# Output stage of an adaLN block: attention numerators loaded in the layout of the product, inverted sums spread over head rows by TensorE

## The chip, the cores and the metric

One Trainium2 chip (trn2); the program runs on 1 core. The metric is the device time of one execution in microseconds (us), the median of three runs.

## The reference, cut to what matters

The block normalises x, runs causal attention with 16 heads of 16 columns, adds a gated attention output to x, and then runs a small mixture-of-experts step on the first two batches. What the change touches is the end of the attention:

```python
B, L, D = 16, 1024, 256          # batches, tokens, columns; 16 heads x 16
probs = softmax(scores)          # the kernel keeps numerators and sums apart
out = einsum('bhij,bhjd->bhid', probs, v)
out = out.transpose(0, 2, 1, 3).reshape(B, L, D)
out = out @ Wo + bo
x = x + ga * (h + out)           # h: the modulated layer norm of x
```

All of it is float32.

## The kernel before, in words

The kernel is a row of blocks, each ended by all engines: `phase0` (tables, weights), `phase1` (norms, q, k, v), `phase2` (scores, exp, weighted sums), `phase3` (the output stage), `phase4` (experts). Only `phase3` changes, with one more tensor in DRAM.

`phase2` leaves `att_d[b, g]`, 128 rows of 1024 tokens for each of four groups of four heads. A head has 32 rows: 16 numerators, then its sum of exponentials (row 16, `DH`), and 15 unused ones. So heads and columns are rows, and tokens are along the free dimension.

`phase3` works through B = 16 batches of T = 8 tiles of 128 tokens. For each batch SyncE loads `gate`, `ob` (three bf16 parts of a bias) and `att` (2 MB, two buffers; L1122 to L1125), and three to four batches ahead x and `a2` (L1127 to L1131). It stores a batch once all eight tiles are added (L1135 to L1137), and issues the next loads behind that store.

Per tile TensorE transposes the four groups of `att` into one PSUM bank, 128 tokens by 512 (L1230). VectorE takes the reciprocal of the 16 sums (L1166) and multiplies the numerators by it into `norm`, 128 by 256 (L1170). TensorE transposes `norm` in two pieces (L1238), ScalarE copies them to `n_t` (L1199), and TensorE adds up a bias matmul (L1248, bf16) and two float32 matmuls of `n_t` with `wg` (L1250). `wg` is `Wo` times the batch's gate, two VectorE products at the batch's start (L1159). VectorE adds the residual (L1177). The residual `res` comes from ScalarE (L1189) and two GpSimd products (L1213, L1215), up to a batch ahead. The three steps of a tile are staggered by one tile each on TensorE, within a batch: the loop over `T + 2` steps starts and ends anew in each batch. A float32 matmul shows as two instructions in the trace, a transposition as one.

The order of the work is written out by hand: each engine has its own queue, and semaphores set who waits.

Of the kernel before, what the change touches and what calls it, by code (L numbers as in the profile page):

```python
# [17 lines left out]
F32 = mybir.dt.float32  # L18
# [3 lines left out]
ALU = mybir.AluOpType  # L22
# [38 lines left out]
def build(nc, a, out):  # L61
# [20 lines left out]
    att_d = nc.dram_tensor("att", [B, NG, P, L], F32, kind="Internal").ap()  # L82
    tok_d = nc.dram_tensor("tok_rows", [SEL, D + E], F32, kind="Internal").ap()
    sum_d = nc.dram_tensor("sum_rows", [SEL + P, D], F32, kind="Internal").ap()

    with ExitStack() as outer:
# [19 lines left out]
        phase3(nc, x, ps, ident, wo, ones3, rsx, nmx, mods_d, out_bias_d, att_d, sum_d, out)  # L106
# [975 lines left out]
def phase3(nc, x, ps, ident, wo, ones3, rsx, nmx, mods_d, out_bias_d, att_d, sum_d, out):  # L1082
# [3 lines left out]
    DH = D // HEADS  # L1086
    SB = (sum_d.shape[0] - P) // L
    PS_A, PS_T, PS_C = 0, 2, 4
    XR = 4
    with ExitStack() as ctx:  # L1090
# [3 lines left out]
        att = sb("att_b", [P, 2, NG, L], F32)  # L1094
        xb = sb("x_b", [P, XR, T, D], F32)
        res = sb("res_b", [P, 2, T, D], F32)
        gate = sb("gate_b", [P, 2, D], F32)
        a2 = sb("a2_b", [P, XR, D], F32)
        ob = sb("ob_b", [3, 2, D], BF16)
        wg = sb("wg", [P, 2, KC, D], F32)  # L1100
        rec = sb("rec", [P, 2, HEADS], F32)
        norm = sb("norm", [P, 2, D], F32)
        n_t = sb("n_t", [P, 2, KC, P], F32)
        x2 = sb("x2", [P, 2, T, D], F32)
        att_in, small_in = pair("p3_att_in"), pair("p3_small_in")
        x_in = tuple(sem(f"p3_x_in{r}") for r in range(XR))
        r_norm, r_mul, r_done = sem("p3_r_norm"), sem("p3_r_mul"), sem("p3_r")
        wg_done = sem("p3_wg")
        at_done, rec_done, norm_done = sem("p3_at"), sem("p3_rec"), sem("p3_norm")
        nt_done, nt_copied = sem("p3_nt"), sem("p3_nt_copied")  # L1110
# [4 lines left out]
        def loop(eng, work):  # L1115
            for p in range(2):
                work(p, 0, p)
            for it in range(1, B // 2):
                for p in range(2):
                    work(it * 2 + p, it, p)  # L1120

        def load(sp, b, p):  # L1122
            sp.dma_start(gate[:, p], mods_d[b, M_GA, :].partition_broadcast(P)).then_inc(small_in[p], DMA)
            sp.dma_start(ob[:, p], out_bias_d[b]).then_inc(small_in[p], DMA)
            sp.dma_start(att[:, p], att_d[b].rearrange("g p t -> p g t")).then_inc(att_in[p], DMA)  # L1125

        def load_x(eng, b):  # L1127
            r = b % XR
            reuse(eng, r_done, (b - XR) * T + T)
            eng.dma_start(xb[:, r], x[b].rearrange("(t p) d -> p t d", p=P)).then_inc(x_in[r], DMA)  # L1130
            eng.dma_start(a2[:, r], mods_d[b, M_A2, :].partition_broadcast(P)).then_inc(x_in[r], DMA)  # L1131

        @block.sync
        def _(sp):
            def store(b, p, dst):  # L1135
                sp.wait_ge(x2_done, b * T + T)
                sp.dma_start(dst.rearrange("(t p) d -> p t d", p=P), x2[:, p]).then_inc(stored[p], DMA)  # L1137

            load(sp, 0, 0)
            load_x(sp, 0)  # L1140
            load(sp, 1, 1)
            for b in range(1, XR):
                load_x(sp, b)
            for b in range(B):
                if b + XR - 1 < B and b >= 1:
                    load_x(sp, b + XR - 1)
                store(b, b % 2, sum_d[b * L:(b + 1) * L] if b < SB else out[b])
                if b + 2 < B:
                    load(sp, b + 2, b % 2)
            for p in range(2):  # L1150
                sp.wait_ge(stored[p], DMA * (B // 2))

        @block.vector
        def _(dve):
            def work(b, half, p):
                dve.wait_ge(small_in[p], half * (2 * DMA) + 2 * DMA)
                reuse(dve, stored[p], half * DMA)
# [3 lines left out]
                for t in range(T + 2):  # L1161
                    if t < T:
                        s = t % 2
                        dve.wait_ge(at_done, b * T + t + 1)
                        heads = ps[:, PS_A + s, :].rearrange("p (h n) -> p h n", h=HEADS)
                        dve.reciprocal(rec[:, s, :].rearrange("p (h o) -> p h o", o=1), heads[:, :, DH:DH + 1]) \  # L1166
                           .then_inc(rec_done, 1)
                        dve.wait_ge(rec_done, b * T + t + 1)
                        reuse(dve, nt_done, b * T + t - 1)
                        dve.tensor_tensor(norm[:, s, :].rearrange("p (h n) -> p h n", h=HEADS), heads[:, :, 0:DH],  # L1170
                                          rec[:, s, :].rearrange("p (h o) -> p h o", o=1).to_broadcast([P, HEADS, DH]),
                                          ALU.mult).then_inc(norm_done, 1)
                    if t >= 2:
                        s = t % 2
                        dve.wait_ge(c_done, b * T + t - 1)
                        dve.wait_ge(r_done, b * T + t - 1)
                        dve.tensor_tensor(x2[:, p, t - 2, :], ps[:, PS_C + s, 0:D], res[:, p, t - 2, :], ALU.add) \  # L1177
                           .then_inc(x2_done, 1)

            loop(dve, work)  # L1180

        @block.scalar
        def _(act):
            def first_norm(b, t):
                p = b % 2
                if t == 0:
                    act.wait_ge(x_in[b % XR], (b // XR + 1) * 2 * DMA)
                    reuse(act, x2_done, b * T - T)
                nc.scalar.activation(res[:, p, t, :], xb[:, b % XR, t, :], ACT.Identity, bias=nmx[:, b, t:t + 1],  # L1189
                                     scale=rsx[:, b, t:t + 1]).then_inc(r_norm, 1)  # L1190

            def work(b, half, p):
                for t in range(T):
                    n = b * T + t + 2
                    if n < B * T:
                        first_norm(n // T, n % T)
                    act.wait_ge(nt_done, b * T + t + 1)
                    reuse(act, c_done, b * T + t - 1)
                    nc.scalar.copy(n_t[:, t % 2], ps[:, PS_T + t % 2, 0:D].rearrange("p (k n) -> p k n", k=KC)) \  # L1199
                      .then_inc(nt_copied, 1)  # L1200

            for t in range(2):
                first_norm(0, t)
            loop(act, work)
# [16 lines left out]
        @block.tensor  # L1221
        def _(pe):
            def work(b, half, p):
                pe.wait_ge(att_in[p], half * DMA + DMA)
                for t in range(T + 2):
                    s = t % 2
                    if t < T:
                        reuse(pe, norm_done, b * T + t - 1)
                        for g in range(NG):
                            ins = pe.transpose(ps[:, PS_A + s, g * P:(g + 1) * P], att[:, p, g, t * P:(t + 1) * P],  # L1230
                                               ident[:, :])
                        ins.then_inc(at_done, 1)
                    if 1 <= t <= T:
                        r = t - 1
                        pe.wait_ge(norm_done, b * T + r + 1)
                        reuse(pe, nt_copied, b * T + r - 1)
                        for k in range(KC):
                            ins = pe.transpose(ps[:, PS_T + r % 2, k * P:(k + 1) * P],  # L1238
                                               norm[:, r % 2, k * P:(k + 1) * P], ident[:, :])
                        ins.then_inc(nt_done, 1)  # L1240
                    if t >= 2:
                        r = t - 2
                        if r == 0:
                            pe.wait_ge(wg_done, b + 1)
                        pe.wait_ge(nt_copied, b * T + r + 1)
                        reuse(pe, x2_done, b * T + r - 1)
                        o = ps[:, PS_C + r % 2, 0:D]
                        pe.matmul(o, ones3[:, :], ob[:, p, :], start=True, stop=False)  # L1248
                        for k in range(KC):
                            ins = pe.matmul(o, n_t[:, r % 2, k, :], wg[:, p, k, :], start=False, stop=(k == KC - 1))  # L1250
                        ins.then_inc(c_done, 1)

            loop(pe, work)


# [368 lines left out]
```

## Time and profile before

| | us |
|---|---|
| median of 3 runs (lowest, highest) | 3128.5 (3128.36, 3128.82) |
| the profiled execution, its own time | 3130.67 |
| its span in the profile | 3128.6 |
| PE / DVE / ACT / POOL busy over the span | 2768.8 / 2213.2 / 1818.1 / 1060.7 |
| `phase3`: first transfer issued / last addition ended | 2501.9 / 2782.6 |

PE is TensorE, PEld its weight loads, DVE VectorE, ACT ScalarE, POOL GpSimd, SP SyncE (SPq its queue of transfers). Times in rows are microseconds from the start of the span unless marked ns. The busy shares are means over stages that have different limits; for a change in one stage its own windows and timeline are what to read.

### The profile page before, as it was taken

Reading aid. Unit: us, or ns where it says so; the run is one execution under the profiler, and the core shown is the slowest. Engines: PE = TensorE matmul, PEld = TensorE weight load, DVE = VectorE, ACT = ScalarE, POOL = GpSimd, SP = SyncE. Lnnn points to the kernel's source line nnn. Section 1 sums busy time; section 2 is a strip of 40 time slices with the busy share of each in tenths; the row PEclk is TensorE's granted clock in tenths of the full one; section 3 lists DMA queues with packets and bytes.
Section 4 is the critical chain, followed back from the end, with each engine's and each line's share of the span. In section 5 each row is a group of like instructions: output and inputs, shape, how many; then the busy total and the mean of one; then the engine's idle time right before and its main releaser. Section 6 shows DMA issues by size and latency. Waiting matters only on the chain. (4 is left out here: it accounts for less than half of the span.)

```text
span 3128.6 us, 48266 instructions
## 1 busy us (share of the span) xinstructions
PE 2768.8 (88%) x17467; PEld 1343.6 (43%) x17467; DVE 2213.2 (71%) x3164; ACT 1818.1 (58%) x3723; POOL 1060.7 (34%) x1294
## 2 busy tenths in 40 slices
PE   1677777669999999999999999999999889957997
PEld 0444444324444444444444444444444267744664
DVE  4999999867777777777777777777777245552221
ACT  1655656507777777777777777777777634421121
POOL 1787778421122111211122112212122166642231
PEclk7899899859999999999999999999999989988999
DMA  3366665663444454444444454445444087752342
GB/s 93 118 195 188 200 200 155 215 132 73 104 92 91 93 104 100 89 89 103 104 90 89 97 104 96 91 90 104 100 92 89 22 286 266 268 189 82 83 115 45
DMA packets 188549, 386.18 MB, mean 123 GB/s; under 512 B 33413, under 2 KB 104485, under 8 KB 175800
## 3 DMA queue, kind: packets, MB, share of 16 engines
q1 hardware_dynamic: 182170, 374.58, 46.7%
q0 software_dynamic: 6144, 8.52, 1.6%
q8 instruction: 141, 2.31, 0.3%
q14 instruction: 94, 0.77, 0.1%
HBM read 240.65 MB, written 144.53 MB: 123 GB/s over the span
## 5 line engine op out<-in xcount | busy, mean ns | idle before, releaser
L922 DVE TENSOR_REDUCE mx<-ps 128x2 f32<-128x1024 f32 (+3 forms) x1216 | 1371.6, 1167 | 397.7 <-PE ps L1010 302.4
L968 ACT ACTIVATE prob<-ps 128x512 f32<-128x512 f32 (+1 forms) x2560 | 1251.7, 560 | 539.8 <-PE ps L1028 531.0
L1003 PE MATMUL ps<-k_rows,q_rows 96*128 96x512 bf16 (+3 forms) x3072 | 910.9, 332 | 47.2 <-DMA k_rows<-k_parts 40.6
L1028 PE MATMUL ps<-q_rows,k_rows 99*128 99x512 bf16 (+3 forms) x3072 | 907.4, 329 | 14.2 <-ACT prob L968 5.8
L861 POOL TENSOR_SCALAR_AFFINE_SELECT prob<-prob 128x512 f32<-128x512 f32 x512 | 318.7, 634 | 1452.9 <-ACT prob L968 1452.9
L1047 PE MATMUL ps<-prob,v_rows 128*32 128x512 f32 (+3 forms) x6144 | 628.8, 497 | 0.0
L1028 PEld LDWEIGHTS ps<-q_rows,k_rows 99*128 99x128 bf16 x3072 | 273.1, 98 | 599.1 <-ACT prob L968 360.0
L1003 PEld LDWEIGHTS ps<-k_rows,q_rows 96*128 96x128 bf16 x3072 | 289.8, 98 | 277.7 <-DVE mx L922 60.8
L1010 PE MATMUL ps<-mask_b,unit_b 128*128 128x128 bf16 (+2 forms) x1408 | 348.6, 248 | 0.0
L666 PE MATMUL ps<-x_t,w_all 128*128 128x512 f32 x512 | 248.5, 631 | 0.0
L1047 PEld LDWEIGHTS ps<-prob,v_rows 128*32 128x32 f32 x6144 | 134.4, 108 | 246.1 <-ACT prob L968 123.3
L655 PE MATMUL ps<-ident,h 128*128 128x128 f32 x256 | 55.2, 317 | 151.2 <-ACT x_t L567 82.5
L628 POOL TENSOR_TENSOR h<-xin,mods_b 128x256 f32<-128x256 f32 x128 | 146.0, 1143 | 106.9 <-ACT xin L552 106.8
L635 POOL TENSOR_TENSOR stage<-rest,stage 128x1024 bf16<-128x1024 f32 x64 | 147.5, 2306 | 35.5 <-ACT stage L588 35.4
L1484 DVE SCALAR_TENSOR_TENSOR y<-ps,gx,gate 128x256 f32<-128x256 f32 x32 | 15.5, 484 | 195.9 <-PE ps L1575 195.9
L1010 PEld LDWEIGHTS ps<-mask_b,unit_b 128*128 128x128 bf16 x1408 | 139.5, 99 | 22.8
L1250 PE MATMUL ps<-wg,n_t 128*128 128x256 f32 x512 | 146.6, 409 | 0.0
L666 PEld LDWEIGHTS ps<-x_t,w_all 128*128 128x128 f32 x512 | 101.8, 207 | 104.1 <-issue 103.2
L1199 ACT COPY n_t<-ps 128x256 f32<-128x256 f32 x128 | 47.5, 371 | 155.2 <-PE ps L1238 155.2
L1177 DVE TENSOR_TENSOR x<-ps,res_b 128x256 f32<-128x256 f32 x128 | 54.4, 425 | 109.5 <-PE ps L1250 109.5
L674 PE MATMUL ps<-w_all,x_t 128*128 128x256 f32 x512 | 126.1, 390 | 3.3 <-ACT v_st L576 2.0
L1213 POOL TENSOR_TENSOR res_b<-res_b,a_b 128x256 f32<-128x256 f32 x128 | 93.0, 727 | 85.2 <-ACT res_b L1189 85.2
(154 smaller groups left out, 2777.6 us busy)
## 6 DMA issues: line engine op xcount, KB each, us to landing
k_rows<-k_parts SPq DMA_DIRECT2D x384, 128.0 KB, 7.3
v_ones<-v_st SPq DMA_DIRECT2D x64, 512.0 KB, 4.3
v_rows<-v_ones SPq DMA_DIRECT2D x64, 512.0 KB, 9.1
att<-o_sb SPq DMA_DIRECT2D x128, 256.0 KB, 2.5
att_b<-att SPq DMA_DIRECT2D x16, 2048.0 KB, 9.9
q_parts<-stage SPq DMA_DIRECT2D x128, 192.0 KB, 3.3
k_parts<-stage SPq DMA_DIRECT2D x128, 192.0 KB, 3.3
q_rows<-q_parts SPq DMA_DIRECT2D x64, 384.0 KB, 4.6
```

What stands on the lines that cost most here:

```text
L628: pool.tensor_tensor(h[:, p, t, :], xin[:, r, t, :], mods[:, r, M_CA1, :], ALU.mult).then_inc(h_mul, 1)
L635: pool.tensor_tensor(parts(n, 2), rest[:, n % 2], parts(n, 1), ALU.subtract).then_inc(lo_done, 1)
L666: ins = pe.matmul(ps[:, PS_QK + c, :], w_all[:, k, c * P:(c + 1) * P], x_t[:, blk, k, :], start=(k == 0), stop=(k == KC - 1))
L674: ins = pe.matmul(o, x_t[:, t // 4, k, t % 4 * P:t % 4 * P + P], w_all[:, k, 2 * D:3 * D], start=(k == 0), stop=(k == KC - 1))
L861: pool.affine_select(out=own, in_=own, compare_op=ALU.is_ge, fill=0.0, base=0, pattern=[[0, HG], [1, P]], channel_multiplier=-1).then_inc( ...
L922: dve.tensor_reduce(dst, src, AX.X, ALU.max).then_inc(a_free, 1)
L968: nc.scalar.activation(prob[:, (g * NPC + i) % RING, h, 0:w], src, ACT.Exp).then_inc(exp_done, 1)
L1003: ins = pe.matmul(ps[:, at, col:col + w], q[0:ROWS, g, h, i * P:(i + 1) * P], k[0:ROWS, g, h, k0:k0 + w], start=(r == 0), stop=True, skip_ ...
L1010: ins = pe.matmul(own, unit_b[:, :], mask_b[:, :].rearrange("p (o n) -> p o n", o=1) .to_broadcast([P, per, P]), start=False, stop=True, s ...
L1028: ins = pe.matmul(ps[:, PS_B + bank(g, n), at:at + w], k[0:AUG, g, h, j * P:(j + 1) * P], q[0:AUG, g, h, q0:q0 + w], start=True, stop=True)
L1047: ins = pe.matmul(ps[32 * h:32 * h + 32, PS_O, col:col + w], v[:, g, j, h, :], prob[:, (g * NPC + i) % RING, h, at:at + w], start=(j == 0) ...
L1250: ins = pe.matmul(o, n_t[:, r % 2, k, :], wg[:, p, k, :], start=False, stop=(k == KC - 1))
```

## The change

Instead of loading all rows of a batch's `att` and turning them twice, the stage loads only the numerators, so that the 256 rows of (head, column) fill 128 partitions twice (`num`, 1 MB in two transfers), and the sums apart (`den`: 16 sums of 1024 tokens as 128 rows of 128). VectorE inverts the sums in one instruction per batch; SyncE stores the inverses to DRAM (`rec_d`) and loads them back as 16 rows of 1024 (`rec`). TensorE multiplies a 0/1 matrix (`head_rows`, 16 by 256) by `rec`, which puts each head's inverse on its 16 rows, 512 tokens per matmul, four per batch, two PSUM banks. VectorE multiplies `num` by that bank into `n_t`, which has the layout that the product wants. The product itself is the same three matmuls per tile, now with four PSUM banks.

The spreads and products of batch b+1 are interleaved with the products of batch b: on TensorE one after every second product, on VectorE one after every second addition. `wg` of batch b+1 is made on VectorE at the start of batch b (before: at its own start), from a `gate` that is still loaded behind the store of batch b-1. SyncE's order is new (the listing has it). ScalarE has only the residual left, whose wait is now per tile. In the diff, removed bodies (printed above) are left out.

```diff
@@ build @@
+    rec_d = nc.dram_tensor("rec_sums", [B, HEADS, L], F32, kind="Internal").ap()
...
@@ phase3 @@
+    HALF = L // 2
+    PS_R, PS_C = 0, 2
+    XR, CR = 4, 4
+    NQ = 2 * KC
...
+        num = sb("num", [P, 2, KC, L], F32)
+        den = sb("den", [P, 2, P], F32)
+        inv = sb("inv", [P, 2, P], F32)
+        rec = sb("rec", [HEADS, 2, L], F32)
+        rows = sb("head_rows", [HEADS, HEADS, DH], F32)
+        n_t = sb("n_t", [P, 2, KC, L], F32)
...
         @block.sync
         def _(sp):
...
+            def load_den(b):
+                reuse(sp, inv_done, b - 1)
+                sums = att_d[b].rearrange("g (h n) t -> (g h) n t", n=2 * DH)[:, DH, :]
+                sp.dma_start(den[:, b % 2, :], sums.rearrange("h (a c) -> h a c", c=P)).then_inc(den_in[b % 2], DMA)
+            def save_inv(b):
+                sp.wait_ge(inv_done, b + 1)
+                sp.dma_start(rec_d[b].rearrange("h (a c) -> (h a) c", c=P), inv[:, b % 2, :]).then_inc(inv_stored[b % 2], DMA)
+            def load_rec(b):
+                sp.wait_ge(inv_stored[b % 2], (b // 2 + 1) * DMA)
+                reuse(sp, spread, (b - 1) * NQ)
+                sp.dma_start(rec[:, b % 2, :], rec_d[b]).then_inc(rec_in[b % 2], DMA)
+            def load_num(b):
+                reuse(sp, norm_done, (b - 1) * NQ)
+                for k in range(KC):
+                    mine = att_d[b, k * NG // KC:(k + 1) * NG // KC].rearrange("g (h n) t -> (g h) n t", n=2 * DH)
+                    sp.dma_start(num[:, b % 2, k, :], mine[:, 0:DH, :]) \
+                      .then_inc(num_in[b % 2], DMA)
+            def load_x(b):
+                r = b % XR
+                reuse(sp, r_done, (b - XR) * T + T)
+                sp.dma_start(xb[:, r], x[b].rearrange("(t p) d -> p t d", p=P)).then_inc(x_in[r], DMA)
+                sp.dma_start(a2[:, r], mods_d[b, M_A2, :].partition_broadcast(P)).then_inc(x_in[r], DMA)
+            def load_small(b):
+                reuse(sp, c_done, (b - 1) * T)
+                sp.dma_start(gate[:, b % 2], mods_d[b, M_GA, :].partition_broadcast(P)).then_inc(small_in[b % 2], DMA)
+                sp.dma_start(ob[:, b % 2], out_bias_d[b]).then_inc(small_in[b % 2], DMA)
+            def store(b):
                 sp.wait_ge(x2_done, b * T + T)
...
+                dst = sum_d[b * L:(b + 1) * L] if b < SB else out[b]
+                sp.dma_start(dst.rearrange("(t p) d -> p t d", p=P), x2[:, b % 2]).then_inc(stored[b % 2], DMA)
+            load_den(0)
+            load_den(1)
+            load_num(0)
+            load_small(0)
+            save_inv(0)
+            load_x(0)
+            load_rec(0)
+            save_inv(1)
+            load_num(1)
+            load_rec(1)
+            load_small(1)
+            load_den(2)
+            load_x(1)
+            load_x(2)
             for b in range(B):
...
                 if b + 2 < B:
...
+                    save_inv(b + 2)
+                if b + 3 < B:
+                    load_den(b + 3)
+                    load_x(b + 3)
+                if b + 2 < B:
+                    load_num(b + 2)
+                    load_rec(b + 2)
+                store(b)
+                if b + 2 < B:
+                    load_small(b + 2)
             for p in range(2):
                 sp.wait_ge(stored[p], DMA * (B // 2))
         @block.vector
         def _(dve):
...
+            def invert(b):
+                dve.wait_ge(den_in[b % 2], (b // 2 + 1) * DMA)
+                reuse(dve, inv_stored[b % 2], b // 2 * DMA)
+                dve.reciprocal(inv[:, b % 2, :], den[:, b % 2, :]).then_inc(inv_done, 1)
+            def scale_weights(b):
+                p = b % 2
+                dve.wait_ge(small_in[p], (b // 2 + 1) * 2 * DMA)
                 for k in range(KC):
                     ins = dve.tensor_tensor(wg[:, p, k, :], wo[:, k, :], gate[:, p, :], ALU.mult)
                 ins.then_inc(wg_done, 1)
...
+            def normalise(b, q):
+                k, half = q % KC, q // KC
+                at = slice(half * HALF, (half + 1) * HALF)
+                if q == 0:
+                    dve.wait_ge(num_in[b % 2], (b // 2 + 1) * KC * DMA)
+                    reuse(dve, c_done, (b - 1) * T)
+                dve.wait_ge(spread, b * NQ + q + 1)
+                dve.tensor_tensor(n_t[:, b % 2, k, at], num[:, b % 2, k, at], ps[:, PS_R + q % 2, :], ALU.mult) \
+                   .then_inc(norm_done, 1)
+            def finish(b, t):
+                n = b * T + t
+                if t == 0:
+                    reuse(dve, stored[b % 2], b // 2 * DMA)
+                dve.wait_ge(c_done, n + 1)
+                dve.wait_ge(r_done, n + 1)
+                dve.tensor_tensor(x2[:, b % 2, t, :], ps[:, PS_C + n % CR, 0:D], res[:, b % 2, t, :], ALU.add) \
+                   .then_inc(x2_done, 1)
+            dve.tensor_copy(rows[:, :, :], ident[0:HEADS, 0:HEADS].rearrange("p (h o) -> p h o", o=1)
+                            .to_broadcast([HEADS, HEADS, DH])).then_inc(rows_done, 1)
+            for b in range(2):
+                invert(b)
+            scale_weights(0)
+            for q in range(NQ):
+                normalise(0, q)
+            for b in range(B):
+                if b + 2 < B:
+                    invert(b + 2)
+                if b + 1 < B:
+                    scale_weights(b + 1)
+                for t in range(T):
+                    finish(b, t)
+                    if t % 2 == 1 and b + 1 < B:
+                        normalise(b + 1, t // 2)
         @block.scalar
         def _(act):
                 p = b % 2
                 if t == 0:
                     act.wait_ge(x_in[b % XR], (b // XR + 1) * 2 * DMA)
-                    reuse(act, x2_done, b * T - T)
+                reuse(act, x2_done, (b - 2) * T + t + 1)
                 nc.scalar.activation(res[:, p, t, :], xb[:, b % XR, t, :], ACT.Identity, bias=nmx[:, b, t:t + 1],
                                      scale=rsx[:, b, t:t + 1]).then_inc(r_norm, 1)
...
+            for b in range(B):
                 for t in range(T):
...
+                    first_norm(b, t)
         @block.gpsimd
         def _(pool):
         @block.tensor
         def _(pe):
...
+            def spread_rec(b, q):
+                k, half = q % KC, q // KC
+                n = b * NQ + q
+                if q == 0:
+                    pe.wait_ge(rec_in[b % 2], (b // 2 + 1) * DMA)
+                reuse(pe, norm_done, n - 1)
+                mine = rows[:, k * (HEADS // KC):(k + 1) * (HEADS // KC), :].rearrange("p h n -> p (h n)")
+                pe.matmul(ps[:, PS_R + q % 2, :], mine, rec[:, b % 2, half * HALF:(half + 1) * HALF],
+                          start=True, stop=True).then_inc(spread, 1)
+            def product(b, t):
+                n = b * T + t
+                if t == 0:
+                    pe.wait_ge(wg_done, b + 1)
+                if t in (0, T // 2):
+                    pe.wait_ge(norm_done, b * NQ + (KC if t == 0 else NQ))
+                reuse(pe, x2_done, n - CR + 1)
+                o = ps[:, PS_C + n % CR, 0:D]
+                pe.matmul(o, ones3[:, :], ob[:, b % 2, :], start=True, stop=False)
+                for k in range(KC):
+                    ins = pe.matmul(o, n_t[:, b % 2, k, t * P:(t + 1) * P], wg[:, b % 2, k, :], start=False,
+                                    stop=(k == KC - 1))
+                ins.then_inc(c_done, 1)
+            pe.wait_ge(rows_done, 1)
+            for q in range(NQ):
+                spread_rec(0, q)
+            for b in range(B):
+                for t in range(T):
+                    product(b, t)
+                    if t % 2 == 0 and b + 1 < B:
+                        spread_rec(b + 1, t // 2)
```

## Rows read from the trace of the kernel before

**Rows 1.** Window, steady part: us, PE PEld DVE ACT POOL busy, PEclk, DMA share, GB/s
```profile
2533.99:2782.56 248.57, 234.02 (x1316) 176.44 (x1314) 140.11 (x391) 101.35 (x237) 168.09 (x234) 1.00 0.73 247
```

**Rows 2.** Timeline of TensorE, one tile: start, us, engine, line
```profile
2539.47 0.60 PE L1230 MATMUL ps<-ident,att_b 128*128 128x128 f32 x4
...
2540.22 0.28 PE L1248 MATMUL ps<-ob_b,ones 3*128 3x256 bf16 x1
...
2540.43 1.13 PE L1250 MATMUL ps<-wg,n_t 128*128 128x256 f32 x4
...
2541.40 0.60 PE L1230 MATMUL ps<-ident,att_b 128*128 128x128 f32 x4
```

**Rows 3.** Timeline at a batch's edge, all engines
```profile
2547.49 0.28 PE L1248 MATMUL ps<-ob_b,ones 3*128 3x256 bf16 x1
...
2548.77 0.28 PE L1248 MATMUL ps<-ob_b,ones 3*128 3x256 bf16 x1
...
2550.14 0.42 DVE L1177 TENSOR_TENSOR x<-ps,res_b 128x256 f32<-128x256 f32 x1 [0.85 <-PE ps L1250]
...
2550.48 0.75 DVE L1159 TENSOR_TENSOR wg<-wo,gate_b 128x256 f32<-128x256 f32 x2
...
2550.59 0.36 SPq L1137 DMA_DIRECT2D sum_rows<-x  x1
...
2551.00 0.58 SPq L1123 DMA_DIRECT2D gate_b<-mods  x1
...
2551.62 1.13 SPq L1124 DMA_DIRECT2D ob_b<-out_bias_parts  x1
...
2551.92 0.44 PE L1238 MATMUL ps<-ident,norm 128*128 128x128 f32 x2 [0.94 <-DVE norm L1170]
```

**Rows 4.** Critical chain, one row; groups by form, three: count | busy us, mean ns | idle
```profile
2875.96 12.03 PE ps L1561 x28
...
L1439 DVE TENSOR_TENSOR same<-ps,idxf 128x512 f32<-128x512 f32 x8 | 5.5, 692 | 0.9 <-PE ps L1538 0.4
...
L266 DVE RECIPROCAL e<-e 16x256 f32<-16x256 f32 x1 | 1.7, 1742 | 0.0
...
L1166 DVE RECIPROCAL rec<-ps 128x16 f32<-128x16 f32 x128 | 32.8, 256 | 13.7 <-PE ps L1230 12.6
```

**Rows 5.** Windows after E = 2683.15; landings of L1137, then of L1125
```profile
2683.15:2687.15 4.00, 3.06 (x22) 2.38 (x21) 2.78 (x9) 1.63 (x4) 1.17 (x2) 1.00 0.78 268
2683.15:2688.15 5.00, 4.06 (x26) 3.07 (x25) 3.62 (x11) 2.24 (x6) 2.15 (x3) 1.00 0.75 232
...
2688.60:2689.10 0.50, 0.50 (x6) 0.49 (x5) 0.29 (x1) 0.00 (x0) 0.50 (x2) 1.00 0.89 98
...
2690.15:2692.15 2.00, 2.00 (x13) 1.56 (x12) 1.11 (x3) 0.94 (x3) 1.72 (x3) 1.00 1.02 422
...
2697.60:2698.10 0.50, 0.50 (x3) 0.09 (x1) 0.09 (x1) 0.01 (x1) 0.50 (x2) 1.00 0.40 135
...
DMA to landing us min/median/max: 4.1/4.8/5.1
...
DMA to landing us min/median/max: 8.3/9.9/14.5
```

**Rows 6.** Timeline of the stage's start, and a window of it
```profile
2501.88 0.32 SPq L1123 DMA_DIRECT2D gate_b<-mods  x1
...
2505.09 0.76 DVE L1159 TENSOR_TENSOR wg<-wo,gate_b 128x256 f32<-128x256 f32 x2 [57.43 <-DMA ob_b<-out_bias_parts]
...
2510.90 1.97 PE L1230 MATMUL ps<-ident,att_b 128*128 128x128 f32 x8 [12.18 <-DMA att_b<-att]
...
2517.38 2.08 PE L1250 MATMUL ps<-wg,n_t 128*128 128x256 f32 x4
...
2523.86 1.13 PE L1250 MATMUL ps<-wg,n_t 128*128 128x256 f32 x4
...
2502.00:2520.00 18.00, 6.80 (x25) 5.39 (x26) 3.23 (x9) 3.10 (x7) 3.98 (x6) 0.51 0.86 310
```

More of the change, by code:

```diff
@@ L105, in build @@
         phase2(nc, B, L, ps, ident, mask, q_d, k_d, v_d, max_d, att_d)
-        phase3(nc, x, ps, ident, wo, ones3, rsx, nmx, mods_d, out_bias_d, att_d, sum_d, out)
+        phase3(nc, x, ps, ident, wo, ones3, rsx, nmx, mods_d, out_bias_d, att_d, rec_d, sum_d, out)
         phase4(nc, a, SB, ps, ident, mask, ones3, mods_d, b2_d, tok_d, sum_d, out)
@@ L1078, in _, with phase3 @@
                 weigh(unit(LAST, NG - 1), i)
-def phase3(nc, x, ps, ident, wo, ones3, rsx, nmx, mods_d, out_bias_d, att_d, sum_d, out):
+def phase3(nc, x, ps, ident, wo, ones3, rsx, nmx, mods_d, out_bias_d, att_d, rec_d, sum_d, out):
     B, L, D = x.shape
@@ L1113, in phase3 @@
         block = ctx.enter_context(nc.Block())
[L1115 to L1131, printed above, removed]
         @block.sync
         def _(sp):
-            def store(b, p, dst):
-                sp.wait_ge(x2_done, b * T + T)
[L1137 to L1143, printed above, removed]
+            def load_den(b):
+                reuse(sp, inv_done, b - 1)
+                sums = att_d[b].rearrange("g (h n) t -> (g h) n t", n=2 * DH)[:, DH, :]
+                sp.dma_start(den[:, b % 2, :], sums.rearrange("h (a c) -> h a c", c=P)).then_inc(den_in[b % 2], DMA)
@@ L1144, in _ @@
+            load_small(1)
+            load_den(2)
+            load_x(1)
+            load_x(2)
             for b in range(B):
-                if b + XR - 1 < B and b >= 1:
-                    load_x(sp, b + XR - 1)
-                store(b, b % 2, sum_d[b * L:(b + 1) * L] if b < SB else out[b])
                 if b + 2 < B:
-                    load(sp, b + 2, b % 2)
+                    save_inv(b + 2)
[8 more added lines that the diff above has]
+                    load_small(b + 2)
@@ L1154, in _ @@
         def _(dve):
-            def work(b, half, p):
-                dve.wait_ge(small_in[p], half * (2 * DMA) + 2 * DMA)
-                reuse(dve, stored[p], half * DMA)
+            def invert(b):
[5 more added lines that the diff above has]
+                dve.wait_ge(small_in[p], (b // 2 + 1) * 2 * DMA)
                 for k in range(KC):
@@ L1160, in work @@
                 ins.then_inc(wg_done, 1)
[L1161 to L1178, printed above, removed]
@@ L1180, in _ @@
-            loop(dve, work)
+            def normalise(b, q):
[7 more added lines that the diff above has]
+                   .then_inc(norm_done, 1)
@@ L1222, in _ @@
         def _(pe):
[L1223 to L1251, printed above, removed]
```

27 lines of the change are left out of this document (4 added, 23 removed).

## The prediction

> **What bounds the kernel now.** I read the windows by stage first. The output stage works from the end of batch 0 (2533.99) to the end of batch 15 (2782.56) with TensorE busy 234.0 of 248.6 us at a granted clock of 1.00 (2.4 GHz, the higher of its two levels), the DMA engines 73%, the other engines 68% or less [rows 1]: 15 batches of 16.57 us each. Nothing of the stages before or after overlaps it, since each stage is a block of its own, so what a batch loses the kernel loses.
>
> Next the timeline of one tile in the steady part. From one tile's first transposition to the next one's there are 1.93 us, and TensorE fills them: transpositions of `att_b`, of `norm`, the bias matmul, and the product, which starts 0.21 after the bias and lets the next float32 matmul start 0.97 later [rows 2]. So bias plus product is 1.18 before a float32 matmul. Where a product follows a product, bias to bias is 1.27 [rows 3]. 8 x 1.93 is 15.4; the other 1.1 is the fill and drain at each batch's edge. Call E the end of a batch's last addition (L1177). The last product begins at E - 1.80, its addition starts 1.38 after it began, and SyncE issues the store at E + 0.03, the gate's load 0.41 later, and `ob_b` 0.62 after that [rows 3]. In the kernel before, that gate is wanted a whole batch later: nobody waits.
>
> **Part by part.** *TensorE.* Gone per batch: 32 transpositions of `att_b` and 16 of `norm`. Added: four matmuls of 512 float32 columns. Fourteen such matmuls (28 passes) take 12.03 us [rows 4], 0.86 each; that these contract over 16 rows and those over 128 I cost at nothing, since a column passes either way (bounds: 0.4, if few rows came at half price, and 1.2). With 0.10 to turn to the bias, 0.96. The order is P0 S P1 P2 S P3 P4 S P5 P6 S P7: four products before a spread (1.18), four before a product (1.27), four spreads: 4.72 + 5.08 + 3.84 = 13.64 us against 16.57. That is TensorE's floor.
>
> *VectorE.* Per batch before: 8 reciprocals, 8 products by them, 8 additions, 2 of `wg`. After: one reciprocal of 128 elements a lane, four products of 512, 8 additions, 2 of `wg`. The reciprocal goes from 256 ns at 16 elements to 1742 at 256 [rows 4], about 6.2 ns an element, so 0.95. The products go by the 128x512 row that reads PSUM, 0.69 [rows 4]. Sum 0.95 + 2.8 + 3.4 + 0.75 = 7.9 us, no bound. *ScalarE* loses its copies. *GpSimd* keeps its products, 168.1 us for some 15 batches [rows 1], 11.2 each, with two batches of room: hidden while a batch is over 12 us. *DMA.* Numerators are 1 MB where `att_b` was 2 MB. Before, a burst moves from E + 0.95 to about E + 14.9 [rows 5]. 1 MB less is 2.5 us at the 422 GB/s at which `att_b` comes [rows 5]; sums, inverses and their way back, 64 KB each in pieces of 512 B or 4 KB, cost some 0.5 us. The burst ends near E + 13, before the next E.
>
> *The wait that is new.* The gate and `ob_b` for batch b+2 are still loaded behind store(b), but VectorE scales the weights of b+2 at the start of batch b+1, which is at once. Behind `scale_weights` in VectorE's queue stand all additions of the batch. TensorE can run four products ahead (four banks) and then needs the first addition. So a batch has a second chain. W is the time from E until both loads have landed. Bounds: below, gate and `ob_b` with nothing in front let VectorE start 3.21 after the gate's issue [rows 6], and the gate's issue is at E + 0.44, so 3.65; above, `att_b`, behind the same two loads and 2 MB long, lands 9.9 after its issue at E + 2.2 [rows 3, 5], so 12.1. Between them, the windows at one boundary: 268 GB/s over the first 4 us are 1.07 MB, the store's 1.05; 232 over the first 5 are 1.16 MB, almost store and gate (1.18); then the rate is as low as 98 around E + 5.7, and 422 from E + 7.0 [rows 5]. The slow part is the gate, one row of 1 KB read for 128 partitions. By the bytes it is through at about E + 5.0, by the end of that low window at E + 5.95. I take 5.4, between them, and 0.8 for the landing, which is what the store takes from its last data (E + 4.0) to its landing, 4.8 [rows 5]. **W = 6.2.** In it hide the fourth product by the inverses (0.69) and the reciprocal (0.95): 1.7 us, which cost nothing until W is below 1.7.
>
> The chain: W 6.2; `wg` 0.75; first addition 0.45; TensorE wakes 0.1; P4 S P5 P6 S until P7 begins, 1.18 + 0.96 + 1.27 + 1.18 + 0.96 = 5.55; its result 1.38; the addition 0.42. Together **14.85 us**, W + 8.65. TensorE would have been ready for P4 at E - 0.53 + 6.82 = E + 6.3 and gets it at E + 7.5: 1.2 us idle. TensorE has a pause of 0.94 at each edge now [rows 3] and keeps its 1.00, so the clock costs nothing; the bound is one batch's work at half clock after the first such pause, 14 us once.
>
> *SyncE.* Its order is longer by four issues a batch (0.4 each), and it waits for the inverses' store before it fetches them. All this falls behind the gate and is wanted a batch later: nothing.
>
> *First batch.* Before, TensorE began at 2510.90 after a long idle, at 1.2 GHz: the mean grant from 2502 to 2520 is 0.51, a product takes 2.08 us at 2517.38 and 1.13 at 2523.86 [rows 6]. It was fast some 12 us after it began. Now sums come in (about 2505.1, by the 3.21 above), are inverted (2506), stored behind numerators and gate (landed about 2510), and fetched behind x and `a_b`: 2.8 + 1.5 + 0.2 + 2.8 + 1.5 us of transfers from 2503.5, so landed about 2514. Four spreads at half clock 6.9, P0 and S 4.3: 2525.2. The rest at full clock: 10.2 to P7, and 1.8: E(0) = 2537.2, **3.3 us later** (bounds 0 and 8).
>
> *Last batch.* No spreads, no gate to wait for: 8 x 1.27 = 10.2, which is **6.4 less** than 16.57.
>
> **Sum.** 14 x (14.85 - 16.57) = -24.1; last batch -6.4; first +3.3: **-27.2 us**. The profiled execution has a span of 3128.6 and took 3130.67; the median of the runs is 3128.5. I take the difference off the median: **3101.3 us**.
>
> **Rivals.**
> 1. *TensorE bounds.* W at most 5.0, for which the byte count speaks, and against it the low window around E + 5.7. Then a batch is 13.64 and the sum 14 x (-2.93) - 6.4 + 3.3 = -44: 3084. Chance 0.15.
> 2. *The numerator load runs at half rate.* Its source is 8 heads of 16 rows, its target 128 partitions. If only half of the DMA engines carried it, it would take 5.0 us for 2.5, and the burst would end near E + 15.5 on those. The next store's data start at 14.85 + 0.95 = 15.8, so the wait would stay as it is; only the first batch pays, 2.5 us, and rival 1 is shut, since a batch cannot be shorter than those engines' 14.6 us. Time 3104. No row here has such a load. The Trainium skill, DMA: Bandwidth & Descriptors, section Why a DMA increments its semaphore by 16 and not by 1, says that a DMA is spread over the largest number of engines up to 16 that divides the slowest dimension of both sides, which here is 8; by that rule this is what happens. Chance 0.2.
> 3. *The gate lands later, though still with a gain.* W 7 to 8, if the landing of a slow load lags more than the store's: W = 7.2 gives 15.85, so 3115. Chance 0.1.
> 4. *Slower.* The place is the same wait in VectorE, the mechanism a transfer queue that is not empty when the store is issued: small pieces, half-rate numerators and the wait for the inverses push the burst past the next E, and the gate stands behind the rest of it. A batch breaks even at 16.79 (14 x 0.22 = 3.1 = 6.4 - 3.3), so it decides from W = 8.14. With W = 9, 17.65 a batch: +15.1 - 3.1 = +12: 3140. For it: the engines are at full share through the burst. Against: some 2 us of room by the count above. Chance 0.08.
> 5. *No change*, W near 8.1: 0.03.
>
> **How the numbers follow.** The forecast keeps 0.44 (W 5.7 to 6.7: 3094 to 3109). A measurement tells 0.2%, some 6 us, from nothing. Faster by more: 0.44 + 0.15 + 0.2 + 0.1 = 0.89; within: 0.03; slower: 0.08. The unknown prices stay inside this but for their far ends: a spread at 0.4 or 1.2 us moves P4 to P7 by two spreads a batch, 14 x 2 x 0.4 = 11 us either way. The range leaves out rival 4, no change, and the far ends of rivals 1 and 3: 3086 to 3117.
>
> **What would show it.** Right: VectorE's `wg` group waits for the `gate_b` or `ob_b` DMA, about 4.5 us in each of 14 batches; stores 14.85 us apart, the last 10.2; spreads 0.86 each; TensorE waits once a batch, before P4, for the addition. Wrong: stores under 14 us apart with TensorE never idle (rival 1); the DMA share above zero when the store is issued, and `num` landing 5 us or more after x (2, 4); the granted clock below 1.00 in the steady part; spreads that cost more than 0.96.

## The result, and the profile after

| | before | after |
|---|---|---|
| median, us (lowest, highest, runs) | 3128.7 (3128.4, 3132.2, 4) | 3189.4 (3172.6, 3203.3, 4) |
| ratio to before, 95% interval | | 1.0184 [1.0157, 1.0211] |
| span of the profiled execution, us | 3128.6 | 3170.9 |

The change makes the kernel slower by some 1.8%, and its executions now differ by 1% among themselves, where those of the kernel before agree within 0.1%. A gain of 27 us was forecast. The profiled execution is the fastest of the four (3172.6), 17 us below their median; what the traces show below accounts for that one alone.

The page of the kernel after, its span, TensorE's busy time and the clock in 40 slices:

```profile
span 3170.9 us, 46305 instructions
...
PE 2806.2 (89%) x16827; PEld 1296.9 (41%) x16827; DVE 2184.4 (69%) x2989; ACT 1780.4 (56%) x3595; POOL 1056.5 (33%) x1294
...
PEclk7898899859999999999999999999999778688998
```

The clock in the page of the kernel before:

```profile
PEclk7899899859999999999999999999999989988999
```

TensorE has fewer instructions and is busy for longer. The slices of the output stage say why: the 32nd to the 35th have 7, 7, 8, 6, where the kernel before has 9, 8, 9, 9.

Windows of the kernel after, columns as in [rows 1]: the first batch, all later ones, then batches 1, 2, 4 and 15 by themselves:

```profile
2504.61:2553.72 49.11, 31.43 (x58) 14.43 (x59) 12.73 (x24) 11.95 (x23) 27.93 (x40) 0.55 0.67 179
2553.72:2825.44 271.72, 259.78 (x711) 131.00 (x709) 102.95 (x219) 60.97 (x105) 153.66 (x217) 0.79 0.57 177
2553.72:2568.25 14.53, 14.03 (x49) 7.32 (x48) 7.51 (x17) 4.59 (x8) 12.43 (x19) 1.00 0.72 224
2568.25:2587.53 19.28, 17.14 (x49) 8.62 (x48) 7.31 (x17) 4.69 (x8) 14.56 (x21) 0.82 0.61 207
2609.00:2635.19 26.19, 26.19 (x49) 12.37 (x50) 7.22 (x17) 4.69 (x8) 11.48 (x16) 0.50 0.45 138
2815.27:2825.44 10.17, 9.71 (x39) 5.75 (x37) 3.99 (x10) 0.00 (x0) 0.00 (x0) 1.00 0.31 103
```

Against [rows 1] the 15 later batches take 271.7 us where they took 248.6, at a mean grant of 0.79 where it was 1.00. But a batch whose clock stays at 1.00 takes 14.53. Six of the 15 are like that, 14.5 to 15.6, mean 14.81. Eight run in whole or in part at 1.2 GHz (a grant of 0.50) and take 172.7 together, 54.2 more than eight times 14.81. Batch 4 is at 0.50 from end to end, with TensorE busy for all of its 26.19 us: it waits for nobody, and so nothing else in the profile looks wrong in it. The last batch takes 10.17. The stage began 2.7 us later here (2504.6; before 2501.9), the first batch is 17.0 longer (49.1 against 32.1), the rest 23.2, and what follows the stage is 0.6 shorter: 42.3, the whole difference of the spans.

What TensorE does where the clock falls, in its timeline:

```profile
2567.93 1.13 PE L1288 MATMUL ps<-wg,n_t 128*128 128x256 f32 x4
2571.20 2.07 PE L1275 MATMUL ps<-rec,head_rows 16*128 16x512 f32 x2 [2.13 <-DMA rec<-rec_sums]
2573.07 0.42 PE L1286 MATMUL ps<-ob_b,ones 3*128 3x256 bf16 x1
2573.41 2.08 PE L1288 MATMUL ps<-wg,n_t 128*128 128x256 f32 x4
...
2592.93 1.13 PE L1288 MATMUL ps<-wg,n_t 128*128 128x256 f32 x4
2595.40 0.37 PE L1286 MATMUL ps<-ob_b,ones 3*128 3x256 bf16 x1 [1.34 <-DVE x L1217]
2595.70 2.08 PE L1288 MATMUL ps<-wg,n_t 128*128 128x256 f32 x4
```

A product of 1.13 us is one of 2.08 after a pause. The first pause, 2.13 us, is a wait for the inverses' load; the second, 1.34 us, is the one that was forecast, for the first addition of a batch, which stands behind the gate. The clock falls during each of them, and is down for 6.8 us at the first and for 47.8 us at the second. It stays up at other pauses of this execution (1.58 us in batch 7, 0.5 to 0.84 in batches 1, 6, 9, 13, 14) and falls within 1.3 us after those of 1.67 and 1.63 in batches 8 and 10, for 3.4 and for 58.0 us. So of the four falls one stands at the wait for an addition and three at waits for the inverses.

The waits of the stage in total (us, times, longest):

```profile
DVE wg L1198 <- DMA ob_b<-out_bias_parts: 74.0, 15, 9.0
...
PE ps L1275 <- DMA rec<-rec_sums: 27.8, 6, 19.9
...
PE ps L1286 <- DVE x L1217: 4.5, 6, 1.3
```

VectorE's wait for the gate is there as forecast, 3.8 to 5.2 us a batch after the first (9.0), and costs TensorE only 4.5 us in all. The wait for the inverses was not forecast: 19.9 us of it is the start, the other five come to 7.9. Why they are late is in the DMA share, here windows of batch 1:

```profile
2556.00:2560.00 4.00, 4.00 (x16) 2.16 (x14) 1.06 (x2) 0.00 (x0) 3.75 (x6) 1.00 0.89 247
2564.00:2568.00 4.00, 4.00 (x16) 1.99 (x14) 1.61 (x4) 1.20 (x2) 3.84 (x6) 1.00 0.52 161
```

The burst ends with about 5 us at a share of 0.52, at 161 GB/s. That is what half of the engines at work would show, as in rival 2. The inverses stand behind the numerators in the queue.

### The profile page after: what moved, and what is told of

It reads as the page before. It is cut to its first block and busy times, and to the rows that moved or that the text cites. A ratio compares the mean times of both kernels' runs of the same rounds, so it can differ in the third digit from the quotient of the medians.

```text
span 3170.9 us, 46305 instructions
## 1 busy us (share of the span) xinstructions
PE 2806.2 (89%) x16827; PEld 1296.9 (41%) x16827; DVE 2184.4 (69%) x2989; ACT 1780.4 (56%) x3595; POOL 1056.5 (33%) x1294
## 5 line engine op out<-in xcount | busy, mean ns | idle before, releaser
L1029 PE MATMUL ps<-q_rows,k_rows 99*128 99x512 bf16 (+3 forms) x3072 | 907.0, 328 | 14.7 <-ACT prob L969 6.1
L1244 ACT ACTIVATE res_b<-x_b,nmx,rsx 128x256 f32<-128x256 f32 x128 | 72.9, 596 | 226.4 <-DVE x L1217 196.3
L1288 PE MATMUL ps<-wg,n_t 128*128 128x256 f32 x512 | 184.9, 495 | 0.0
L1288 PEld LDWEIGHTS ps<-wg,n_t 128*128 128x128 f32 x512 | 108.4, 235 | 66.0 <-issue 48.2
```

What stands on the lines that cost most here:

```text
L1029: ins = pe.matmul(ps[:, PS_B + bank(g, n), at:at + w], k[0:AUG, g, h, j * P:(j + 1) * P], q[0:AUG, g, h, q0:q0 + w], start=True, stop=True)
L1288: ins = pe.matmul(o, n_t[:, b % 2, k, t * P:(t + 1) * P], wg[:, b % 2, k, :], start=False, stop=(k == KC - 1))
```

## The experiments

Two theories. **A, pauses:** TensorE's waits let the clock fall, and without them it stays at 1.00. **B, few rows:** the spreads, which contract over 16 rows of the array, let it fall and keep it down. All times are medians, unless one execution is named; the ratios are to runs of the kernel before on the same chip. A build's batches are read from its one traced execution.

### The gate's wait alone

```diff
-        gate = sb("gate_b", [P, 2, D], F32)
+        gate = sb("gate_b", [P, 4, D], F32)
...
+                    load_small(b + 2)
                 store(b)
-                if b + 2 < B:
-                    load_small(b + 2)
```

> Edit: gate and bias parts get four buffers each and are loaded ahead of the store of the batch before, so VectorE never waits for them. Theory A (pauses): the granted clock falls to 1.2 GHz at TensorE's pauses, and there are two kinds, for the gate (0.5 to 1.3 us in each batch) and for the inverses (1.6 to 2.1 us in some batches). This takes away the first kind alone: falls remain at the waits for the inverses; batches at full clock 13.6 to 14 us, total 3110 to 3165. Theory B (few rows): the spreads, which contract over 16 rows, keep the clock low whatever the pauses: the mean grant of the stage stays near 0.79 and the total at 3165 to 3200.

3173.2 us, ratio 1.0124 [1.0096, 1.0151]: in total this is outside what theory A gave (3110 to 3165) and inside what B gave (3165 to 3200). VectorE no longer waits for the gate, and batches without a fall take 13.97. But the inverses' load is late in every second batch, by more than before. That fits shorter batches that leave the half-rate numerators less time, which was not tested by itself. Windows of batches 1 and 2:

```profile
2547.76:2561.73 13.97, 13.97 (x49) 7.32 (x48) 7.87 (x17) 4.69 (x8) 13.27 (x20) 1.00 0.77 224
2561.73:2582.23 20.50, 16.84 (x49) 8.58 (x48) 7.90 (x17) 4.80 (x8) 18.30 (x26) 0.83 0.60 200
```

Each of its six pauses (2.4 to 4.0 us) comes with a fall, and the clock falls nowhere else: where it falls is as theory A has it. How long it stays down is not: 6.8 us four times, but 20.5 and 58.0 at the two others, and that makes the total.

### All DMA engines for the numerators

```diff
-                    sp.dma_start(num[:, b % 2, k, :], mine[:, 0:DH, :]) \
+                    sp.dma_start(num[:, b % 2, k, :], mine[:, 0:DH, :].rearrange("h n t -> n h t")) \
```

`Wo` and `head_rows` get the same order of rows.

> Edit: the numerators' rows are ordered (column, head) instead of (head, column), with Wo and the 0/1 matrix in the same order, so that the slowest dimension of the source is 16 and not 8. If the half share of the DMA engines (0.50 for 4 to 5 us at the end of each burst) comes from the 8, it goes, the burst ends near E + 12.5, and the inverses land before they are wanted: no wait of 1.6 to 2.1 us. The gate's wait stays (0.5 to 1.3 us per batch). Theory A: the clock falls in a few batches only; total 3100 to 3150. Theory B: mean grant near 0.79, total 3160 or more.

3159.1 us, ratio 1.0086 [1.0069, 1.0103]: between the two forecasts. Two stretches of batch 2 and the whole of it:

```profile
2562.02:2576.48 14.46, 14.05 (x49) 7.32 (x48) 6.94 (x17) 4.59 (x8) 11.32 (x17) 1.00 0.89 247
2564.00:2568.00 4.00, 4.00 (x15) 1.93 (x13) 0.27 (x1) 0.00 (x0) 2.93 (x5) 1.00 0.89 248
2570.00:2574.00 4.00, 4.00 (x15) 2.10 (x14) 2.53 (x7) 2.31 (x5) 3.76 (x6) 1.00 1.01 270
2574.00:2576.00 2.00, 2.00 (x8) 0.84 (x7) 0.26 (x1) 0.60 (x1) 1.92 (x4) 1.00 0.99 227
```

The half share is gone, so the 8 as the outer dimension of the source was its cause. The waits for the inverses are shorter (0.4 to 1.7 us) but not gone: they still come last in the queue. The clock falls four times, after pauses of 0.41, 0.69, 1.69 and 1.59 us (batches 4, 8, 10, 13), and not after those of 1.28, 1.00 and 0.97 (batches 3, 7, 11): the length of a pause does not by itself decide.

### Both

> Edit: both of the above. Theory A: no pause of TensorE in the steady part, grant 1.00 from batch 1 on, batches of 13.64 us (TensorE's floor), total E(0) near 2546 plus 14 x 13.64 plus 10.2 plus 345.5 for the rest: 3093 us. Theory B: grant still near 0.8 or lower, batches of 14 to 26 us, total above 3150.

3118.6 us (3102 to 3138 in ten runs), ratio 0.9953 [0.9930, 0.9975]: faster than the kernel before, but neither forecast. The gate's wait is gone, and the inverses' is 0.3 to 1.75 us in some batches. The clock fell in batch 4 (grant 0.74), whose only pause of more than a quarter of a microsecond was 0.59 us, and in batch 8 (0.82), after 1.75 us. It was also late to rise at the start: TensorE worked 41 us without a gap before it did.

### Rows alone

```diff
-        rec = sb("rec", [HEADS, 2, L], F32)
-        rows = sb("head_rows", [HEADS, HEADS, DH], F32)
+        rec = sb("rec", [P, 2, L], F32)
+        rows = sb("head_rows", [P, HEADS, DH], F32)
```

Rows 16 to 127 of `rec` are set to 1 once, those of `head_rows` to 0, so that they add nothing to the sums.

> Edit: the changed kernel, but the spread contracts over 128 rows: 112 more rows with weight 0 and data 1, the same result and columns. Theory A: nothing changes, since the pauses stay: 3165 to 3200. Theory B: the clock stays at 1.00 in the steady part and rises soon at the start: batches of 14.5 to 14.9 us, total 3095 to 3115. A mixture: the falls at the pauses stay, but the time at 1.2 GHz after each is shorter (12 us instead of up to 58): 3115 to 3150.

3135.2 us, ratio 1.0007 [0.9994, 1.0019]: the mixture. Nothing was taken out of the change but the 16; the matmuls pass the same columns, and 1.8% comes back. (The two traces are 25 us apart and not 54, since the traced execution here, 3147.4 us, is the slowest of ten, and that of the changed kernel the fastest of four.) Its pauses are even longer than in the changed kernel (six of 2.8 to 4.6 us for the inverses). The stretch after one of them:

```profile
2654.00:2660.00 6.00, 6.00 (x13) 3.04 (x12) 2.11 (x5) 1.20 (x2) 1.79 (x3) 0.51 0.91 273
2660.00:2669.41 9.41, 9.41 (x35) 5.03 (x33) 3.73 (x9) 3.00 (x5) 7.90 (x12) 1.00 0.31 97
```

A fall comes with each of the six long pauses and lasts 6.8 us, once 10.2; another of 6.8 comes after a pause of 2.4 in the first batch. None follows the pauses of 0.4 to 1.4 us.

### Both waits and rows

> Edit: gate loaded early, numerators on 16 engines, spread over 128 rows. The runs so far say that both theories hold in part: a pause lets the clock fall, and matmuls over 16 rows let it fall at smaller pauses and keep it down. By this mixture: pauses of 0.3 to 1.8 us for the inverses remain in some batches, none below 1.2 us lets the clock fall; batches of 14.0 to 14.6 us at 1.00, E(0) 2546 to 2549, total 3090 to 3105. If pauses alone counted, as the kernel without the 128 rows: 3102 to 3138.

3095.5 us, ratio 0.9886 [0.9870, 0.9903], inside the forecast by the mixture. Batch 1 has a pause of 2.8 us and a fall of 3.4 us; from batch 2 on there are pauses of 0.3 to 1.0 us and no fall. This build differs from the one under "Both", 3118.6 us, by the rows alone. The stretch from TensorE's first instruction of the stage to the rise of its clock, with 16 rows (that build) and with 128:

```profile
2517.87:2559.26 41.39, 41.39 (x72) 19.11 (x73) 14.21 (x25) 13.42 (x26) 35.95 (x51) 0.50 0.67 188
```

```profile
2521.06:2525.44 4.38, 4.38 (x5) 1.77 (x6) 1.28 (x2) 3.64 (x8) 3.86 (x6) 0.50 1.04 220
```

### Inverses first

```diff
+                    load_rec(b + 2)
                     load_num(b + 2)
-                    load_rec(b + 2)
```

with the early gate and the 16 engines, with 16 rows and with 128.

> Edit: gate loaded early, numerators on 16 engines, and the inverses fetched before the numerators instead of after them. No wait is left in the steady part. If pauses alone let the clock fall: grant 1.00 from batch 1 on, 13.97 us a batch, total near 3092. If matmuls over 16 rows do so without any pause: some batches at 0.6 to 0.8 with no idle time before, total 3105 to 3140.

> Edit: the same with the spread over 128 rows. Both theories: no pause, grant 1.00 in all steady batches, 13.97 us each; the clock at the start rises some 12 us after TensorE begins as in the kernel before; E(0) 2542 to 2547; total E(0) + 14 x 13.97 + 10.2 + 345.5 = 3093 to 3098, and the scatter between executions is under 0.3%.

3096.7 us, ratio 0.9902 [0.9878, 0.9925], with 16 rows; 3085.8, ratio 0.9860 [0.9844, 0.9876], with 128. Batches 1 to 13 of each:

```profile
2542.45:2724.10 181.65, 181.65 (x625) 95.15 (x624) 100.52 (x196) 61.04 (x104) 157.53 (x221) 1.00 0.92 252
```

```profile
2536.38:2713.18 176.80, 176.80 (x625) 99.61 (x624) 102.39 (x197) 60.93 (x104) 162.05 (x227) 1.00 0.95 260
```

No pause, no fall, with 16 rows too, so few rows alone do not bring the clock down in this trace. One of the four executions with 16 rows took 3108.0; it has no trace, and its reason is open. With 128 rows the four are within 0.16%. The kernel with 128 rows is also faster in the steady part, 13.60 a batch to 13.97. That was not forecast: its total lies below the 3093 to 3098 expected. Of the other 6 us most is the start, where the clock is down 17.1 us and not 27.3. Where the 13.97 comes from stands in TensorE's and its weight loads' timeline, 16 rows first:

```profile
2615.49 1.13 PE L1293 MATMUL ps<-wg,n_t 128*128 128x256 f32 x4
2616.55 1.12 PE L1280 MATMUL ps<-rec,head_rows 16*128 16x512 f32 x2
...
2616.55 0.29 PEld L1280 LDWEIGHTS ps<-rec,head_rows 16*128 16x128 f32 x2 [0.33 <-DVE n_t L1210]
```

```profile
2621.06 1.13 PE L1297 MATMUL ps<-wg,n_t 128*128 128x256 f32 x4
2622.03 1.02 PE L1284 MATMUL ps<-rec,head_rows 128*128 128x512 f32 x2
...
2621.82 0.41 PEld L1284 LDWEIGHTS ps<-rec,head_rows 128*128 128x128 f32 x2
```

Product to spread is 1.06 us with 16 rows and 0.97 with 128: the weights of 128 rows are loaded 0.2 us ahead, beside the product, those of 16 rows only when it is over. (The multiplication named in the bracket is not what it waits for: the first spread of each batch, where the last `n_t` was done 3.6 us before, starts just as late.) Four times 0.09 is 0.36 of the 0.37 a batch.

### Three bf16 parts

Against the build above with 128 rows:

```diff
-                dve.reciprocal(inv[:, b % 2, :], den[:, b % 2, :]).then_inc(inv_done, 1)
...
-        rec = sb("rec", [P, 2, L], F32)
+        rec = sb("rec", [P, 2, L], BF16)
```

VectorE splits the reciprocal into three bf16 numbers whose sum it is to within rounding; they fill 48 rows of `rec`, and the other rows are set to 1 against weights of 0.

> Edit: as before, but the inverses are split into three bf16 parts on 48 rows (four more VectorE instructions a batch) and each spread is one bf16 matmul of 512 columns, over 128 rows of which 80 have weight 0. A spread falls from 0.86 to 0.22 us, TensorE's floor from 13.97 to 11.4; GpSimd's 16 instructions (11.9 us a batch) become the bound and the transfers (12.5 us a burst) nearly so. If the clock holds: 12.5 us a batch, total 3065 to 3080. If TensorE's shorter pauses for the additions let the clock fall: 3080 to 3130.

3085.2 us, ratio 0.9850 [0.9833, 0.9866]. Its batches 1 to 13, where TensorE is busy 87% of the time:

```profile
2539.04:2718.13 179.09, 155.94 (x573) 90.13 (x572) 132.68 (x248) 59.65 (x104) 160.96 (x224) 0.93 0.93 261
```

Undisturbed batches take 12.0 to 12.2 us, but TensorE waits 0.9 to 2.2 us for an addition in each, and in five of the thirteen the clock falls, for 3.4 or 6.8 us: at pauses of 1.7 to 2.2 us, while three others of 1.6 to 2.0 leave it up. A TensorE that is busy for 12% less gains nothing: the second of the two forecasts. It also shows that spreads over 128 rows do not protect from every short pause.

### One pause, put in

The question left was whether the slow stretches of 47.8 and 58.0 us are the price of one pause or of many. Into kernels without falls in their steady part, one pause is put in batch 3 and one in batch 9:

```diff
+                if b in (3, 9) and t == 4:
+                    pe.wait_ge(hold, (b // 3 // 2 + 1) * DMA)
```

`hold` comes from two small loads that ScalarE issues one after the other once product 3 is done (in the kernel before, once it has copied `n_t` of tile 2).

> Edit: the kernel whose inverses come first (16-row spreads, no wait left, 1.00 throughout), with one pause of TensorE put in before the fifth product of batches 3 and 9: it waits there for two small loads one after the other, about 4 to 5 us. If a pause is what makes the clock fall and few-row matmuls are what keeps it down: a fall at each pause, and more than 15 us at 1.2 GHz after it. If the long slow stretches of the changed kernel came from its repeated pauses alone: back within 12 us.

> Edit: the same two pauses, spreads over 128 rows. A fall at each pause; back within 7 to 12 us by either theory. If it too stays down for longer, rows are not the reason.

> Edit: the kernel before, with the same two pauses of TensorE before the fourth tile's step of batches 3 and 9 (two small loads, one after the other). Its matmuls over few rows are the bias alone. A fall at each pause and a return within 7 to 12 us: then what the old kernel was spared was the pause. No fall: then its mix of matmuls holds the clock through pauses that the new one does not survive.

> Edit: as the 128-row kernel with the two pauses, but the 112 added rows carry data 0 as well as weight 0. If the chip goes by what an instruction covers: as with data 1, back within 12 us. If it goes by values that change: as with 16 rows, longer, and batches without a pause may fall as well.

One execution each: 3154.8, 3111.5, 3154.5 and 3109.8 us. The loads took twice what I had expected, and the pauses 7.8 to 9.9 us. What is compared is how long TensorE then works at 1.2 GHz. Restart, and a window over the slow stretch from it (the rise of the clock lies within 0.2 us of its end), with 16 rows, with 128, and in the kernel before:

```profile
2591.18 0.37 PE L1301 MATMUL ps<-ob_b,ones 3*128 3x256 bf16 x1 [9.87 <-DMA spot<-out_bias_parts]
...
2591.18:2625.50 34.32, 34.32 (x64) 16.64 (x65) 9.11 (x18) 6.00 (x10) 13.64 (x20) 0.50 0.39 105
```

```profile
2582.30 0.37 PE L1305 MATMUL ps<-ob_b,ones 3*128 3x256 bf16 x1 [8.97 <-DMA spot<-out_bias_parts]
...
2582.30:2585.50 3.20, 3.20 (x7) 1.92 (x7) 0.42 (x1) 0.33 (x1) 3.04 (x5) 0.50 0.00 0
```

```profile
2585.22 1.11 PE L1238 MATMUL ps<-ident,att_b 128*128 128x128 f32 x4 [8.39 <-DMA spot<-out_bias_parts]
...
2585.22:2590.50 5.28, 5.28 (x18) 3.83 (x18) 1.59 (x5) 0.96 (x3) 1.45 (x2) 0.50 0.11 36
```

| pause in batch 3, 9 | clock down, us | of it after the restart |
|---|---|---|
| spreads over 16 rows | 41.0, 47.8 | 34.2, 40.9 |
| over 128, added data 1 | 10.2, 13.7 | 3.4, 6.1 |
| over 128, added data 0 | 10.2, 13.7 | 3.9, 6.2 |
| kernel before | 10.2, 10.2 | 5.3, 4.7 |

(The clock falls during the pause; the last column leaves the pause out.) One pause is enough for a slow stretch of 40 us and more, with TensorE busy without a gap from its restart on, and the builds with 16 and with 128 rows differ in nothing but the spreads' rows: it is the 16 that keep the clock down. Weight and data of the added rows may both be 0: here the rows that the instruction covers make the difference, and not what is in them.

## Why the prediction was wrong

The forecast was faster, with 0.89, and 3101; it came out 3189. The slower case had 0.08, by another mechanism (a full transfer queue), and none of the rivals had the clock. The profiled execution is 69.5 us above the forecast (42.3 longer where 27.2 less was said): 53.7 of it lie in the fifteen later batches, 16.4 in the first batch and its start, and what follows the stage is 0.6 shorter. For the other 17 us up to the median there is no trace.

- *The steady batch.* The chain was right where the clock stayed up, but that the mean comes out so near, 14.81 us against 14.85, is partly luck: five of the six batches take 14.65 in the mean, since their W was 5.2 to 6.1, and the sixth 15.63, by a wait for the inverses that was not in the sum. Behind W came 8.75 us in four of the five, against 8.65 in the sum. W was 5.2 to 6.6 against 6.2, TensorE's wait before the fifth product 0.5 to 1.3 against 1.2, the reciprocal 0.94 against 0.95, the product of 512 0.68 against 0.69, the last batch 10.17 against 10.2. With 14 batches of 14.81 and one of 10.17 the fifteen are 217.5 us, 31 less than before. The floor said 13.64; it is 13.97 with 16 rows and 13.60 with 128.
- *"so the clock costs nothing".* This is the step that failed. It held a pause of 1.2 us against one of 0.94 that leaves the clock alone in the kernel before, and took the mix of matmuls for equal. The eight batches that fell cost 54.2 us, which turns -31 into +23. One of the four falls stands at the very pause that was forecast (1.34 us, 47.8 down); three stand at the inverses' waits, which were put at nothing. In the kernel before the pause of 0.94 sits among transpositions and matmuls over 128 rows, with three rows in the bias alone; the experiments show both parts, the pause that lets the clock fall and the 16 rows that keep it down. The bound that I gave, 14 us once, supposed a quick return after one fall.
- *"contract over 16 rows and those over 128 I cost at nothing".* From a spread to the next bias it took 0.96 us, as forecast, but the rows have a price of two other kinds: 0.09 us at each turn from product to spread, and the clock. The kernel with 128 rows and nothing else changed is at 1.0007.
- *"wanted a batch later: nothing"* (SyncE's order). The inverses for batch b+2 are fetched last of a burst and wanted one batch on, just after the next E; I counted the burst, and not that this load is the last in it. Five waits of 0.9 to 2.1 us, 7.9 in all, before what the clock makes of them.
- *Rival 2* has its mechanism, shown by the half share and by its end with the 16. The Trainium skill, DMA: Bandwidth & Descriptors, section Why a DMA increments its semaphore by 16 and not by 1, gives a transfer the largest number of engines up to 16 that divides the slowest dimension of both sides. The trace agrees: a share of 0.52 with 8, and 0.89 to 1.01 with 16. But "the wait would stay as it is" looked at the gate alone. It delays the inverses, and so brings pauses.
- *The first batch.* 35.3 us forecast from the first issue, 49.1 measured: TensorE began 16.8 after it, not 12.1, and the clock rose 29 us after that, not 12. The kernel before needed 12 us of its own mix; I carried that number over to another mix. Over the runs the clock rises 15 to 41 us after TensorE begins with spreads over 16 rows, and 3.7 to 5.5 us after with float32 spreads over 128.

What the changed layout is worth once the gate comes early, the inverses come first, the numerators take all engines and the spreads cover 128 rows is shown by the last build with float32 spreads: 0.9860 [0.9844, 0.9876], some 45 us.

Not settled: what decides whether a short pause lets the clock fall. With 16 rows it fell after 0.41 us in one build and stayed up at 1.58 in the changed kernel; with three bf16 parts it fell at 1.67 and stayed up at 1.96. Nor whether the chip goes by the rows or by something that comes with them, such as the 0.09 us at each turn from product to spread: no run separates the two. And it is not rows alone: the build with three bf16 parts, its spreads over 128 rows, needed 14.7 us at the start for its clock to rise. Where the scatter between the executions goes is open as well, since only one of each has a trace, and so is whether a number of rows between 16 and 128 would do.

## What to carry to other kernels

A change that takes work off TensorE and leaves it with short waits can cost more than it saves, because the work that remains may run at half clock (here 54 us lost against 31 saved): look for every new wait of TensorE, not only for those on the longest chain, and for matmuls that use few rows. When a stage is slower with TensorE busy all the time, read the granted clock by batch first; rows of weight 0 that fill up a small contraction cost no columns, and here brought the change from 1.0184 back to 1.0007. Look at the outer dimension of a transfer too (a DMA share of 0.52 with 8, 0.89 and more with 16), and the load that stands last in a burst is the one to check against its due time.

## What the runs showed of the hardware that was not expected

- After one pause of 9 to 10 us, TensorE worked 34 and 41 us without a gap at a grant of 0.50 when four of its 28 matmuls of a batch contracted over 16 rows, and 3.4 and 6.1 us when the same four covered 128. Weights and data of 0 in the added rows did as well as data of 1 (3.9 and 6.2 us).
- At the start of the stage, after 16 us and more without work, the clock rose 15 to 41 us after TensorE began with the 16-row spreads (six traces) and 3.7 to 5.5 us after with float32 spreads over 128 (five traces).
- The weights of a 16-row float32 matmul are not loaded ahead beside a 128-row one: 1.06 us from product to spread, 0.97 with 128 rows.
- Two 1.5 KB loads, issued by ScalarE one after the other beside SyncE's burst, let TensorE go on 8.9 to 9.8 us after the first was issued; the first alone took 4.6 to 7.5.
